# Layer 0 of a two-layer FFN kernel in batch slots, its second transpose done by DMA from ScalarE's queue

## The reference, cut to what matters

```python
h = relu(x @ w1[lang] + b1[lang])                   # 256 -> 64
y = x + h @ w2[lang] + b2[lang]                     # 64 -> 256
z = layernorm(y) * gamma[lang] + beta[lang]
# two BitNet linears: ternary weights, 8-bit per-token codes
g = gelu(bitlinear(z, W1, b1))                      # 256 -> 1024
x = x + bitlinear(g, W2, b2)                        # 1024 -> 256
```

## Time and profile before

| | us |
|---|---|
| median of 3 runs | 352.84 (352.76 to 355.46) |
| the profiled execution | 355.09 |
| its span, first to last instruction | 353.3 |
| mean granted clock of TensorE | 0.966 |
| PE busy | 282.5 (80% of the span) |
| DVE busy | 300.3 (85%) |
| ACT busy | 225.9 (64%) |
| POOL busy | 252.4 (71%) |

### The profile page before, as it was taken

One profiled execution on the slowest core, in us unless ns is written; L12 is line 12 of the kernel. 1 busy time (PEld: TensorE's weight loads), 2 busy tenths in 40 slices (PEclk: granted clock), 3 DMA queues, 4 the chain that ended last, 5 costly groups with the idle time before them and its releaser, 6 DMA issues.

```text
span 353.3 us, 6776 instructions
## 1 busy us (share of the span) xinstructions
PE 282.5 (80%) x1880; PEld 192.2 (54%) x1880; DVE 300.3 (85%) x649; ACT 225.9 (64%) x301; POOL 252.4 (71%) x429
## 2 busy tenths in 40 slices
PE   0628779999999999979567879989797989868683
PEld 0216336565656555646444557767585766646462
DVE  0773987999999999995879889999999999999682
ACT  3255556667667676776415679687778777777570
POOL 2252276766677767774579989999898989899701
PEclk9999989999999999999969898999999999999699
DMA  8982224252423343116007104675657574455765
GB/s 223 230 289 88 67 70 128 89 137 97 128 98 128 105 122 123 66 50 219 31 16 242 42 2 117 86 201 144 156 151 194 148 182 119 113 127 117 143 149 129
DMA packets 63211, 44.74 MB, mean 127 GB/s; under 512 B 40373, under 2 KB 56509, under 8 KB 63174
## 3 DMA queue, kind: packets, MB, share of 16 engines
q1 hardware_dynamic: 58934, 39.89, 42.1%
q10 hardware_dynamic: 4240, 4.41, 4.6%
HBM read 27.51 MB, written 8.39 MB: 102 GB/s over the span
## 4 chain that ended last, share of the span: by engine, by line
PE 36%; issue 21%; POOL 18%; DVE 14%; DMA 7%; ACT 2%; ACTq 1%; DVEq 0%; POOLq 0%
PE banks L1245 8%; POOL mid L745 6%; PE banks L1222 6%; PE banks L1178 5%; POOL xb L728 4%; PE banks L1223 3%; PE banks L1236 3%; POOL raw_all L752 3%; DMA raw_all<-in_w2b 3%; PE banks L1190 3%; DVE amy L1022 3%; DMA convb<-in_convb 2%; DVE xb L1016 2%; DMA q1T<-r 2%; DVE xb L1040 1%
## 5 line engine op out<-in xcount | busy, mean ns | idle before, releaser
L708 POOL TENSOR_SCALAR r<-g,qs 128x1024 f32<-128x1024 f32 x32 | 35.9, 1122 | 44.6 <-DVE qs L993 44.1
L752 POOL TENSOR_TENSOR raw_all<-raw_all,mid 128x1024 f32<-128x1024 f32 x32 | 63.8, 2005 | 0.2 <-DVE raw_all L1047 0.2
L563 ACT ACTIVATE banks<-xb,taps 128x512 f32<-128x512 f32 x64 | 43.7, 690 | 22.6 <-DVE xb L1040 22.5
L529 ACT ACTIVATE g<-banks,dqz 128x1024 f32<-128x1024 f32 x32 | 35.5, 1109 | 31.6 <-PE banks L1223 30.2
L745 POOL TENSOR_SCALAR mid<-xb,taps,convb 128x512 f32<-128x512 f32 x64 | 49.4, 779 | 0.2 <-DVE xb L1040 0.2
L1047 DVE SCALAR_TENSOR_TENSOR raw_all<-xb,taps,banks 128x512 f32<-128x512 f32 x64 | 45.8, 741 | 0.0
L1040 DVE TENSOR_TENSOR xb<-banks,dqb 128x512 f32<-128x512 f32 x64 | 43.0, 688 | 1.8 <-PE banks L1349 1.7
L978 DVE TENSOR_REDUCE am<-g 128x1 f32<-128x1024 f32 x32 | 38.7, 1208 | 6.5 <-ACT g L529 6.5
L1376 PE MATMUL banks<-tern,q1T 128*128 128x256 bf16 x256 | 34.9, 281 | 8.7 <-DMA q1T<-r 4.0
L1349 PE MATMUL banks<-yT,tern 128*128 128x512 bf16 x128 | 35.9, 392 | 7.0 <-ACT yT L549 3.5
L1053 DVE TENSOR_REDUCE am<-g 128x1 f32<-128x1024 f32 x32 | 38.9, 1215 | 1.8 <-ACT g L569 1.8
(11 more groups left out here) (104 smaller groups left out, 574.0 us busy)
## 6 DMA issues: line engine op xcount, KB each, us to landing
xT<-in_xT SPq DMA_DIRECT2D x8, 512.0 KB, 3.6
xtok<-in_x SPq DMA_DIRECT2D x8, 512.0 KB, 3.6
x_after_layer<-x SPq DMA_DIRECT2D x16, 256.0 KB, 2.4
x<-x_after_layer SPq DMA_DIRECT2D x8, 512.0 KB, 4.0
xr<-x_after_layer SPq DMA_DIRECT2D x8, 512.0 KB, 3.7
out_y<-o SPq DMA_DIRECT2D x32, 128.0 KB, 2.0
wl<-in_cwl SPq DMA_DIRECT2D x8, 256.0 KB, 3.4
raw_all<-in_w1a ACTq DMA_DIRECT2D x1, 1024.0 KB, 5.0
```

What stands on the lines that cost most here:

```text
L563: act.activation(bank(BANK_U[g % 3]), apad[:, f, 2:S + 2], ACT.Copy, scale=taps[:, f, 2:3]).then_inc(p_last, 1)
L752: pool.tensor_tensor(c[:, 2 * q:2 * q + 2, :], c[:, 2 * q:2 * q + 2, :], mid[q % 2][:, :, :], ALU.add).then_inc(p_sum, 1)
```

## The change

Layer 0 is written anew in slots of a whole batch, as layer 1 was. `slot1(s)` runs for s = 0 to 11 on every engine; a batch b is begun in slot b and finished in slots b + 3 and b + 4. The start (weights, identities, bias) and the seam are put into the same slots by `once(s, at, op)`. In detail:

- `transpose1` leaves PE: it is a DMA transpose, issued from ACT's queue (`act.dma_start_transpose`), of a tile's codes, which are now 16-bit integers with an offset of 128. There are four buffers for the codes (`r1`), two for the transposed ones (`q1T`). `untranspose` on ACT is gone. `down1` has one more matmul a tile, with the column sums, as in layer 1.
- `statistics` and `mean_variance` leave DVE. `add_adapted` is two `scalar_tensor_tensor` with a sum output; POOL makes the negative mean, and ACT computes the sum of squares in `squares`, two Square activations with a sum output a pair.
- `round1` of the first tile of a batch moves from POOL to ACT.
- x, xT, the adapter, gamma and beta are double-buffered.
- SP issues xT first and loads all weights but the first; `ternary(2)` and `ternary(3)` run in slots 2 and 4, not in the seam.
- PSUM bank 7 is free of transposes and takes `adapter_in`.

The diff, cut to its core (after the buffers ScalarE, then VectorE's `add_adapted`, then TensorE):

```diff
+        r1 = [sb(f"r1_{k}", [P, H], U16) for k in range(TB)]
         q1T = [sb(f"q1T{k}", [P, KH, P], BF16) for k in range(2)]
...
-            def untranspose(c_, k):
-                n, par, h = c_
-                act.wait_ge(s_t1[k], n + 1)
-                wait(act, s_dn[k], n)
-                act.activation(q1T[k][:, :, :].rearrange("p k c -> p (k c)"),
-                               bank16(BANK_T1, F16)[:, :], ACT.Copy, bias=-OFFSET).then_inc(s_q1T[k], 1)
+            def squares(b, p):
+                act.wait_ge(s_nmean, pair(b, p))
+                wait(act, s_rstd, pair(b - 1, p))
+                for k in range(2):
+                    ins = act.activation(squares_out[2 * p + k], xx[p][:, k, :], ACT.Square, bias=nmean[p][:, k:k + 1],
+                                         accum_out=ssq[p][:, k:k + 1])
+                ins.then_inc(s_ssq, 1)
+            def transpose1(b, j):
+                act.wait_ge(s_r1[j], b + 1)
+                wait(act, s_dn, tile(b, j - 2))
+                act.dma_start_transpose(q1T[j % 2][:, :, :].bitcast(U16), r1[j][:, :]).then_inc(s_q1T[j], 16)
...
+            def slot1(s):
+                once(s, B + 2, lead, 0, 1)
+                on(adapter_hidden, s)
+                on(gelu, s - 3, 3)
+                on(transpose1, s - 3, 1)
+                once(s, B, lead, 0, 0)
+                on(round_z, s - 2, 1)
+                on(squares, s - 1, 1)
+                once(s, 3, weight_sum, 3)
+                on(transpose1, s - 3, 2)
+                on(gelu, s - 2, 0)
+                on(untranspose_z, s - 2, 1)
+                once(s, 0, weight_sum, 0)
+                once(s, 0, identities)
+                once(s, B + 3, lead_scales, 0)
+                on(gelu, s - 2, 1)
+                on(transpose1, s - 3, 3)
+                once(s, 1, weight_sum, 1)
+                on(round1, s - 2, 0)
+                on(round_z, s - 1, 0)
+                on(squares, s, 0)
+                once(s, 1, weight_sum, 2)
+                on(gelu, s - 2, 2)
+                on(transpose1, s - 2, 0)
+                on(untranspose_z, s - 1, 0)
...
+            def add_adapted(b, p):
+                dve.wait_ge(s_admm, pair(b, p))
+                dve.wait_ge(s_ldx[b % 2], 16 * (b // 2 + 1))
...
+                for k in range(2):
+                    ins = dve.scalar_tensor_tensor(out=xx[p][:, k, :], in0=bank(BANK_AD)[:, k * D:(k + 1) * D],
+                                                   scalar=1.0, in1=xtok[b % 2][:, 2 * p + k, :], op0=ALU.mult,
+                                                   op1=ALU.add, accum_out=sums[p][:, k:k + 1])
...
+            def down1(b, j):
...
+                pe.wait_ge(s_q1T[j], 16 * (b + 1))
+                wait(pe, s_x1, tile(b, j - 1))
+                for c in range(KH):
+                    pe.matmul(o, q1T[k][:, c, :].bitcast(F16), w_dn0[:, c, :], start=(c == 0), stop=False)
+                ins = pe.matmul(o, uncode[:, :], colsum[1][:, :], start=False, stop=True)
+                ins.then_inc(s_dn, 1)
+            def slot1(s):
+                on(adapter_out, s - 1, 1)
+                once(s, B + 3, transpose_y, 0)
+                on(transpose_z, s - 2, 0)
+                once(s, B + 1, transpose_x, 0, 1)
+                on(adapter_in, s)
+                on(down1, s - 4, 3)
+                once(s, B, transpose_x, 0, 0)
+                once(s, B + 2, linear, 0, 0)
+                on(up1, s - 2, 0)
+                once(s, 1, weight_total, 1)
+                on(down1, s - 3, 0)
+                on(transpose_z, s - 2, 1)
+                once(s, 2, weight_total, 2)
+                on(up1, s - 2, 1)
+                once(s, B + 2, linear, 0, 1)
+                on(down1, s - 3, 1)
+                on(adapter_out, s, 0)
+                once(s, B + 2, spread_scales, 0)
+                once(s, 0, weight_total, 0)
+                on(up1, s - 2, 2)
+                once(s, 3, weight_total, 3)
+                on(down1, s - 3, 2)
+                on(up1, s - 2, 3)
```

More of the change, by code:

```diff
@@ L288, in on, with once, tile, pair @@
                 op(b, *k)
-        def run(slot, seam, slot2, eng, after=()):
-            for k in range(6):
-                slot(k // 2, k % 2)
-                if k in after:
-                    after[k]()
-            for i in range(3, B - 1):
-                slot(i, 0)
-                slot(i, 1)
-            slot(B - 1, 0)
-            slot(B - 1, 1)
+        def once(s, at, op, *k):
+            if s == at:
+                op(*k)
+        def tile(b, j):
+            return TB * b + j + 1
+        def pair(b, p):
+            return PAIR * b + p + 1
+        def before(sem_of, b, j, n):
+            m = len(sem_of)
+            return (sem_of[j - n], b + 1) if j >= n else (sem_of[j - n + m], b)
+        def run(slot1, seam, slot2):
+            for s in range(B + 4):
+                slot1(s)
             seam()
@@ new lines, in gelu, with round1 @@
+            def gelu(b, j):
+                p = j // 2
+                act.wait_ge(s_up, tile(b, j))
+                act.wait_ge(s_dqz, pair(b, p))
+                wait(act, *before(s_r1, b, j, 2))
+                act.activation(g1[j % 2][:, :], bank(BANK_UP + 2 * (j % 2), 2), ACT.Gelu,
+                               scale=dqz[p][:, j % 2:j % 2 + 1]).then_inc(s_gelu, 1)
+            def round1(b, j):
+                act.wait_ge(s_qs1, tile(b, j))
+                wait(act, s_q1T[j], 16 * b)
+                act.activation(r1[j][:, :], g1[j % 2][:, :], ACT.Copy, scale=qs1[j % 2][:, 0:1],
+                               bias=CODE).then_inc(s_r1[j], 1)
@@ L580, in seam @@
             def seam():
[L581 to L590 removed]
+                pass
             def slot2(s):
@@ L798, in slot2 @@
                 on(scale_of_down, s - 2, 2)
-            run(slot, seam, slot2, pool)
+            run(slot1, seam, slot2)
         @block.vector
@@ L1095, in seam @@
+            def seam():
                 pads()
-                final1(pair(PAIRS - 1), 0)
-                final1(pair(PAIRS - 1), 1)
                 dequant(0, 0)
```

951 lines of the change are left out of this document (382 added, 569 removed).

## The result

366.13 us (median of 4 runs, 364.38 to 369.70) against 353.99 for the kernel before on the same chip: ratio 1.035 [1.026, 1.045]. The forecast was 333.0, the range 326 to 346. The profiled execution took 364.38 us, its span 362.6.

The account below looks back on a forecast made before the run. It took PE to bound layer 0, DVE layer 1, and only order the seam. At 14.9 us a batch the first `dequant` moves from 184.7 to 164.8, so 352.84 - 19.9 = 333.0 us, range 326 to 346.

Parts of the forecast that it names:

- Transpose to `down1`: Layer 0: a transpose lands in 3.1 us, 4.5 at most; `down1` comes 4.2 to 7 us after issue, so it is hidden.
- transposes land late: Rival, layer 0's two buffers: a landing of 6.5 us eats the gain, 7.5 gives period 19.2 and 372 us; chance 0.09.
- The period: Middle of layer 0: DVE 14.5, PE 14.4, plus 0.4 of waits, so 14.9 us a batch instead of 16.74.
- ACT's issues: Layer 0: DMA issues mostly hidden, ACT 12.9 us; rival: each holds ACT 1.24 us, 341.4 us in all, chance 0.17.
- The orders that do not mesh: Rival, slots 2 to 10: chains of waits cost 2.1 us each, 352 us, no change; chance 0.08.
- The start: Batch 0's `add_adapted` begins at 15.4 us instead of 17.1, as PE's first adapter no longer waits for ACT's identities.
- slot 0: First slot of layer 0: DVE's list takes 11.0 us, with one ternary pass at 3.9.
- the ternary passes: DVE, slots 2 and 4: each pass over one weight adds 3.9 us (1.50 + 2.44).
- The drain: From batch 7's start to layer 1's first `dequant`: stays near 43 us.
- The rest: From layer 1's first `dequant` to the end: unchanged at 168.6 us.

Follow-up runs that it names:

- x5: The change with tiles 2 and 3 of a batch transposed by TensorE, tiles 0 and 1 by DMA: 352.96 us, 0.996 of the kernel before.
- x6: The change with tiles 0 and 1 of a batch transposed by TensorE, tiles 2 and 3 by DMA: 367.28 us, 1.036 of the kernel before.
- x1: The change with loads of x and xT cut to 16 and 8 columns from batch 2 on: 346.51 us, 0.980 of the kernel before.
- x10: x5 with the loads at the head of the slot and POOL's second residual moved up: 361.88 us, 1.023 of the kernel before.
- x16: x12 with the two ternary passes over layer 1's weights in slots 8 and 9 instead of 2 and 4: 348.78 us, 0.987 of the kernel before.
- x4: The change with four buffers for the transposes' outputs instead of two: 361.62 us, 1.022 of the kernel before.
- x11: x9 with four buffers for the transposes' outputs instead of two: 365.92 us.
- x12: x5 with the loads for layer 1 moved behind a store in SP's list: 349.18 us, 0.988 of the kernel before.
- x9: The change with the loads at the head of the slot and POOL's second residual moved up, all transposes by DMA: 365.99 us.
- x2: The change with layer 0's transposes issued from SP's queue, between the loads, instead of ACT's: 370.06 us, 1.046 of the kernel before.
- x7: x5 with 14 idle matmuls put back at the start: 356.29 us, 1.005 of the kernel before.

## Why the prediction was wrong

**The step that failed** is "Transpose to `down1`": "So the landing is hidden, by 1.1 us at the tightest place." The landing of 3.1 to 4.5 us was taken from layer 1, where SP issues transposes and loads in one list. Issued from ACT's queue beside SP's burst of loads, it took 4.9 to 12.0 us (T2: 12.0, 10.7, 9.9, 7.9, 11.5, one per slot). The room was 4.2 to 7, and the 1.1 us held for the median alone: layer 1's own worst landing, 4.5, was already above the tightest room of 4.2. x5 against x6 (same DMA work, other tiles: 14 us) shows that the meeting does it; x1 (no loads: 20 us less) and x10 against x5 (other place of the loads: 9 us, the landings being a part) agree. The step asked how long a landing takes and where it is needed; it laid the orders of PE and ACT side by side, but not SP's, and so did not ask what SP issues in that interval.

**The landings do not hold all of the miss.** Of the 33.1 us between forecast and measurement x1 gives back 19.6. It still reaches the first `dequant` 10.1 us after the forecast: 4.4 us in slots 0 to 2, 2.6 in slots 3 to 6, 2.7 in the drain and 0.4 at the start; and its rest is 2.6 us longer. So with the landings on time the forecast would still have been some 13 us too low.

**The rival "transposes land late"** named this place and, at 7.5 us, a period of 19.2 and 372 us; measured are slots of 18 to 26 us and 366.1. It had 0.09. It was judged by the mean DMA share, and the case against it was layer 1's worst landing. The engines were busy 15.7 us a slot (0.73 of 21.6), where it had 13.5 at most; the share stayed below its 0.91 because the slots grew. But the share decides little: x6 at 0.56 has late landings, x16 none in slots of 0.60 to 0.74. Its mechanism, two buffers, holds at most 4.5 us of the loss (x4), and nothing in x11, so that 366 lies near its 372 is in part luck. By its own formula it lengthens a period of 14.9 from a landing of 5.4 us on; 6.5 is where the whole gain is gone.

The page "DMA: Bandwidth & Descriptors" of the Trainium skill (section "Issuing engines are not separate DMA queues") says that DMAs of different issuers share 16 engines and interleave. The trace agrees: 3.1 us alone, 9.9 beside SP's loads, with packets of both queues on the engines. The prediction drew from it that ACT's queue is no better than SP's here, and then took layer 1's landings, in SP's one list, for SP's queue as such.

**The period.** Forecast 14.9; 14.78 in x16, with two tiles on PE. That they agree is luck: the forecast had DVE as the longest, in x16 it is PE with two tiles' transposes, and the parts were less good than their sum. DVE: forecast 14.5, measured 13.2. The sum output is a second instruction as the page "VectorE: DVE Perf Modes" of the Trainium skill (section "Two Vector instructions with no wait between them") says, but `add_adapted` and its read take 0.35 us from one start to the next (83.21, 83.56, 83.91 in the changed kernel), so 0.70 for two and not 0.80 + 0.25; that is 0.7 us a batch, and the other 0.6 of the overestimate I have not traced. PE: 14.4 forecast; x16's 14.78 holds two groups of transposes of some 0.5 each, which leaves 13.8. POOL: 11.3 forecast, 12.6 measured (37.74 over three slots). ACT: 11.5 forecast before the issues, 11.2 measured.

**ACT's issues** were hidden for the larger part, as assumed. ACT in order of time in the changed kernel:

```profile
97.78 1.10 ACT L501 ACTIVATE g<-banks,dqz 128x1024 f32<-128x1024 f32 x1
98.34 1.25 ACTq L513 DMA_TRANSPOSE q1T<-r  x1
99.69 0.51 ACT L483 ACTIVATE rz<-z,qsz 128x256 f32<-128x256 f32 x1 [0.81 <-issue]
```

The issue begins inside the gelu ahead and leaves 0.81 us of idle time, not the 0.25 of the forecast and not the 1.24 of the rival. At 82.40 one took 3.18 us and left 2.96 idle. ACT was never the limit, 11.2 of 21 us, but T1's issue stands in the chain with 1.25 us a slot.

**The orders that do not mesh** hold a smaller part: slots 1 and 2 take 17.0 and 17.8 where 15.0 and 17.2 were forecast, also in x1. **The start** was 14.7 (forecast 15.4), **slot 0** 12.7 (11.0), **the ternary passes** 3.1 to 3.3 a slot in x16 (3.9). **The drain** was 42.8 (42.9), but 44.4 to 50.6 us in the versions with shorter slots: in x5 a store behind layer 1's loads takes over 4 us of it (x12). Why the change does not pay for that store is not shown. **The rest** was 170.7 (168.6).

## What to carry to other kernels

A DMA on the path is costed by what is in flight in its interval, not by its own landing elsewhere: lay the orders of all issuing queues side by side with it, and give a burst from another queue a slot of its own before a second queue carries something an engine waits for. Where several small transfers of a slot move to DMA, move only those that meet no burst: two of four tiles gave 353.0 us (349.2 with late loads for layer 1) where all four gave 366.1 and none 358.8. That is no more than 1.2% under the kernel before, of the 5.6% forecast. Count the clock too: the matmuls behind a long wait ran at half clock. A list of loads ahead of a store stalls whoever reuses the store's buffer.

## What the runs showed of the hardware

- A DMA transpose of a 128 x 1024 tile lands in 3.0 to 3.1 us alone, with all 16 engines busy for 1.4 us of them. Issued while another queue sent loads of 1.9 MB within 8 us it took 4.9 to 12.0 us (the change; T2 7.9 to 12.0).
- How full the DMA engines are on the mean did not tell whether landings were late: late at a share of 0.56 (x6), 4.2 us at most at 0.60 to 0.74 (x16, slots 4 to 6).
- The issue itself stretched too: 1.25 us at the median, 2.4 to 3.0 for four of x9's T2, issued 2.6 to 2.8 us behind T1.
- In one queue, behind the loads of x, gamma and beta, it landed in 3.0 to 4.9 us between 60 and 150 us (x2), counted from its issue; xT was sent only after the transposes there.
- An operation of DVE with a sum output is followed by a record of 0.08 us; the pair takes 0.35 us from start to start, less than the 0.40 of `final1`, an operation of the same kind without a sum output.
- Behind waits of 6.9, 4.5 and 4.2 us for a transpose the granted clock stood at its lower level, 1.2 GHz, for a part of TensorE's next matmuls, behind one of 1.8 us it did not: the same pieces took 5.88 us at a mean of 0.55 and 3.32 at 1.00 (the change).
- The granted clock of a stretch can read 1.00 at the start of a span while matmuls take their time at half clock: four of `adapter_in` 3.65 us at 21.67 in x7, 1.93 at 93.67.
